# Cross-attention weighs both halves of a pair of heads in one group every second step

## The reference

```python
x = x + attn(layernorm(x), Wq, Wk, Wv, Wo)      # 32 heads of 16, 8 groups of keys, causal
x = x + xattn(layernorm(x), ctx, ctx)           # the change lies here
x = x + ffn(layernorm(x), w_gate, w_up, w_down) # 512 -> 2048 -> 512, weights -1, 0, 1, activations rounded to 8 bits

def xattn(q, k, v):            # all (4, 512, 512); 8 heads are cut from the middle axis
    qh, kh, vh = (a.reshape(32, 64, 512) for a in (q, k, v))
    qk = einsum('bdm,bdn->bmn', qh, kh) / 8
    sm = softmax(qk, axis=-1)
    return einsum('bmn,bcn->bcm', sm, vh).reshape(4, 512, 512)
```

## Time and profile before

| | |
|---|---|
| median of 3 runs | 859.85 us (857.26 to 863.59) |
| profiled execution | 858.61 us |
| its span, first to last instruction | 856.5 us |
| granted TensorE clock, mean | 0.968 |
| TensorE (PE) busy | 770.8 us, 90% |
| VectorE (DVE) busy | 658.1 us, 77% |
| ScalarE (ACT) busy | 468.2 us, 55% |
| GpSimd (POOL) busy | 412.1 us, 48% |

### The profile page before, as it was taken

One profiled execution on the slowest core, in us unless ns is written; L12 is line 12 of the kernel. 1 busy time (PEld: TensorE's weight loads), 2 busy tenths in 40 slices (PEclk: granted clock), 3 DMA queues, 4 the chain that ended last, 5 costly groups with the idle time before them and its releaser, 6 DMA issues.

```text
span 856.5 us, 14217 instructions
## 1 busy us (share of the span) xinstructions
PE 770.8 (90%) x4258; PEld 407.6 (48%) x4306; DVE 658.1 (77%) x1934; ACT 468.2 (55%) x823; POOL 412.1 (48%) x412
## 2 busy tenths in 40 slices
PE   2999679999999999998887699999996998999996
PEld 1888424444444444443665345544443343444442
DVE  7555288888898989882677787888885788889883
ACT  3556317676676767676222466666664543444451
POOL 1456379999991000001222187777787444333331
PEclk9999859999999999999999699999998999999999
DMA  7996464444342121200457455556552034443443
GB/s 257 348 329 251 131 198 117 153 148 138 128 115 55 58 61 48 72 25 20 160 191 239 134 167 159 160 168 170 158 165 59 13 69 99 98 87 87 87 86 99
DMA packets 112268, 113.61 MB, mean 133 GB/s; under 512 B 70592, under 2 KB 82496, under 8 KB 109120
## 3 DMA queue, kind: packets, MB, share of 16 engines
q1 hardware_dynamic: 105344, 91.66, 38.2%
q0 software_dynamic: 1728, 12.58, 4.3%
q10 hardware_dynamic: 5120, 8.46, 2.7%
HBM read 81.26 MB, written 20.51 MB: 119 GB/s over the span
## 4 chain that ended last, share of the span: by engine, by line
PE 16%; DVE 14%; issue 7%; POOL 5%; DMA 4%; SPq 4%; ACT 2%; DVEq 0%; ACTq 0%; POOLq 0%
PE r_pn L1235 3%; PE r_p L1278 3%; DMA r_rden<-inverse_sums 3%; POOL r_h L905 3%; DVE r_h L1097 2%; DVE r_mx L1058 2%; PE r_p L1223 2%; PE r_p L1198 2%; DVE r_stats L1024 2%; PE r_p L1224 2%; DVE r_hpart L1105 2%; PE r_pn L1294 1%; PE r_pd L1245 1%; DVE r_lo L1032 1%; DVE tok L1038 1%
## 5 line engine op out<-in xcount | busy, mean ns | idle before, releaser
L576 DVE CUSTOM_DVE_ANT_0 b_junk<-b_p,mask_qk 128x128 bf16<-128x128 f32 (+3 forms) x512 | 218.0, 484 | 35.0 <-PE b_p L601 34.8
L531 ACT ACTIVATE b_probs<-b_p 128x512 f32<-128x512 f32 (+1 forms) x352 | 176.8, 560 | 49.8 <-remote 23.8
L601 PE MATMUL b_p<-b_ks,b_qs 96*128 96x128 bf16 (+3 forms) x512 | 127.8, 314 | 19.1 <-DMA b_ks<-k_parts 11.1
L630 PE MATMUL b_p<-b_qs,b_ks 98*128 98x512 bf16 (+1 forms) x352 | 123.3, 365 | 2.0 <-DMA b_qs<-b_mrow 0.9
L948 ACT ACTIVATE r_probs<-r_p 128x512 f32<-128x512 f32 x128 | 74.3, 593 | 65.8 <-PE r_p L1224 63.7
L1058 DVE TENSOR_REDUCE r_mx<-r_p 128x1 f32<-128x512 f32 x128 | 84.9, 685 | 14.6 <-PE r_p L1198 13.4
L879 POOL TENSOR_TENSOR r_halves<-r_probs 128x1024 f32<-128x1024 f32 x32 | 76.6, 2393 | 25.6 <-ACT r_probs L948 23.2
L601 PEld LDWEIGHTS b_p<-b_ks,b_qs 96*128 96x128 bf16 x512 | 45.5, 100 | 82.8 <-DVE b_mx L576 20.0
L645 PE MATMUL b_pv<-b_probs,v 128*32 128x512 f32 (+3 forms) x1024 | 75.5, 436 | 0.0
L855 POOL MEMSET r_ql<- 64x2048 f32 x1 | 1.8, 1799 | 144.6 <-POOLq L402 144.6
L1278 PE MATMUL r_p<-wu,r_zt 128*128 128x512 bf16 x251 | 65.8, 382 | 5.0 <-DVE r_h L1097 4.8
(11 more groups left out here) (149 smaller groups left out, 1552.9 us busy)
## 6 DMA issues: line engine op xcount, KB each, us to landing
r_k<-in_ctx SPq DMA_DIRECT2D x64, 128.0 KB, 2.7
r_qh<-x_normed_high SPq DMA_DIRECT2D x64, 128.0 KB, 2.8
q_parts<-a_parts SPq DMA_DIRECT2D x16, 384.0 KB, 3.5
b_qs<-q_parts SPq DMA_DIRECT2D x32, 192.0 KB, 3.2
a_x<-in_x SPq DMA_DIRECT2D x4, 1024.0 KB, 5.6
a_wst<-in_w_gate SPq DMA_DIRECT2D x4, 1024.0 KB, 6.4
a_wst<-in_w_up SPq DMA_DIRECT2D x4, 1024.0 KB, 7.9
a_wst<-in_w_down SPq DMA_DIRECT2D x4, 1024.0 KB, 8.4
```

The source lines that it names most:

```text
L531: nc.scalar.activation(pblock(j % 2, kb)[:, j0:j0 + nj, c:c + w], p2[(NE * j + n) % BANKS2][:, 0:nj * w].rearrange("p (j c) -> p j c", j=n ...
L576: best = nc.vector.tensor_tensor_reduce(out=junk[:, 2 * ((NU * i + k) % BANKS1) + n, 0:w], in0=bank[:, c:c + w], in1=keep["mask_qk"][:, SE ...
L601: last = nc.tensor.matmul(p1_bank(i, k)[:, c:c + w], qs[0:STACK, s, j, qt * P:(qt + 1) * P], ks[0:STACK, s, 0:w], start=True, stop=True)
L630: last = nc.tensor.matmul(bank, ks[0:STACK + 2, s, kb * P:(kb + 1) * P], qs[0:STACK + 2, s, j0:j0 + nj, kb * P + c:kb * P + c + w], start= ...
```

## The change

Before, in even steps (2p + 6) TensorE sums the pair and weighs its key blocks 0 and 1, in odd steps (2p + 7) it weighs blocks 2 and 3. After, all four blocks are weighed in step 2p + 6, and odd steps weigh nothing. The same matmuls run with the same operands, into the same bank and in the same order among themselves; `weighted` is signalled at the end of step 2p + 6 in place of 2p + 7. No other engine's program changes.

```diff
-                first_half, second_half = pair_due(i, 6), pair_due(i, 7)
-                if first_half is not None:
-                    sum_probs(first_half)
-                    weigh(first_half, 0)
-                    weigh(first_half, 1)
-                if second_half is not None:
-                    weigh(second_half, 2)
-                    weigh(second_half, 3)
+                p = pair_due(i, 6)
+                if p is not None:
+                    sum_probs(p)
+                    for nb in range(KD):
+                        weigh(p, nb)
```

## The result

The changed kernel takes 874.23 us (median of 6 runs, 870.93 to 878.80) against 860.26 (6 runs, 857.26 to 863.59). The ratio is 1.0165, 95% interval 1.0124 to 1.0207: slower by 14 us. The prediction said 873.

A forecast was written before the change was run, and what follows sets the result against it. Bound: a loop per pair of steps, VectorE's maxima up to the transpose, then TensorE alone. Moved weighing 23.9 - 1.6 - 8.9 = +13.4 us on 859.85 gives 873; 8-in-10 range 861.5 to 882.

The forecast's parts named there:

- Part two: Even step's transpose of row maxima to next odd step's first score matmul: 5.01 to 6.72 us, costing 23.9 us in all.
- Part one with the y product: Odd step's first score matmul to the transpose, steps 11 to 31: 5.5 us, subtraction clear of GpSimd, saving 8.9 us.
- Part one without it: First score matmul to transpose in steps 7 and 9, before any y product: 5.0 us, saving 1.6 us.
- The end: Steps 33 to 37, transpose of step 33 to the next scores: taken as 0, about 1 us either way.
- The odd step's subtraction: Rival: VectorE's subtraction still meets GpSimd and stays slow, +20.8 us, 881; chance 0.20, including half the pairs.
- TensorE's clock: Rival: idle gaps drop TensorE to 1.2 GHz in some pairs; three such pairs give 17 us, about 890; chance 0.04.
- Hidden anyway: Rival: a VectorE and GpSimd loop of about 11.3 us covers the moved block; +0 to +4, about 862; chance 0.19.
- faster: Rival: the transpose does not hold TensorE, pairs become pure TensorE work; 7 us won, 853; chance 0.07.
- the prediction's two cases: Odd step's subtraction in steps 11 to 31 running alone, +13.4 us in total, or beside GpSimd, +20.8 us.

The follow-up runs named there:

- e2: Kernel before with three key blocks weighed in the even step and one in the odd step; 862.71 us, ratio 1.0043.
- e5: Kernel before with GpSimd's work on the sums cut (halves adds 128 of 512 columns, total two key blocks); 855.75 us, ratio 0.9943.
- e1: Kernel before with key blocks 2 and 3, the odd step's half of the weighing, left out; 862.36 us, ratio 1.0030.
- e8: Kernel before with key blocks 0 and 1, the even step's half of the weighing, left out; 852.99 us, ratio 0.9936.
- e3: Kernel before with one key block weighed in the even step and three in the odd step; 856.86 us, ratio 0.9974.

## Why the prediction was right

*Part two.* Forecast 5.01 + 1.71 = 6.72 us, measured 6.69 to 6.74 in all twelve pairs. e2 gives the same price per block, 0.85 us.

*Part one with the y product.* Forecast 5.5 us, measured 5.48 to 5.50 in steps 11 to 31. The reason given holds: GpSimd's total ended 0.8 us before the subtraction, as worked out, and e5 shows that GpSimd was the cause of the 6.26 us before.

*Part one without it.* Forecast 5.0 us for steps 7 and 9, measured 5.86 and 5.28. This term was mis-sized, because of a dependency that the prediction did not have. It named the mrow DMA as what the even step's first second_scores waits for. The trace names ScalarE's copy of kh, the high part of the context rows for the second of the two matmuls; it is a stage of step j + 2 that the list of stages ahead doesn't have. ScalarE's and TensorE's timelines of the changed kernel, steps 19 and 20:

```profile
580.83 0.62 ACT L983 ACTIVATE r_kh<-r_kk 64x512 fp32r<-64x512 f32 x1
...
581.55 0.47 PE L1223 MATMUL r_p<-r_qh,r_kk 128*128 128x512 f32 x1 [0.76 <-ACT r_kh L983]
...
582.33 0.27 PE L1207 MATMUL r_p<-ident,r_mx 128*4 128x128 f32 x1
```

The copy is written behind three exponentials of the odd step; it ends at 581.45 and the matmul starts 0.1 us later. With a y product VectorE's last maximum is later still (its row starts at 581.59, the transpose at 582.33), so it costs nothing there; without one it decides. What makes the copy late, and step 7 longer than step 9, are two DMAs of `den` that ScalarE itself issues in front of the third exponential (L974). ScalarE and its queue, then TensorE, in step 7, and behind the second mark ScalarE and its queue in step 9:

```profile
505.56 1.27 ACTq L974 DMA_DIRECT2D r_few<-r_den  x1
506.87 0.63 ACTq L974 DMA_DIRECT2D r_few<-r_den  x1
507.55 0.60 ACT L948 ACTIVATE r_probs<-r_p 128x512 f32<-128x512 f32 x1 [1.01 <-PE r_p L1224]
508.04 0.62 ACT L983 ACTIVATE r_kh<-r_kk 64x512 fp32r<-64x512 f32 x1
...
508.76 0.47 PE L1223 MATMUL r_p<-r_qh,r_kk 128*128 128x512 f32 x1 [1.42 <-ACT r_kh L983]
...
518.19 0.66 ACTq L974 DMA_DIRECT2D r_few<-r_den  x1
518.88 0.63 ACTq L974 DMA_DIRECT2D r_few<-r_den  x1
519.55 0.60 ACT L948 ACTIVATE r_probs<-r_p 128x512 f32<-128x512 f32 x1 [0.39 <-PE r_p L1224]
```

The third exponential starts 0.04 to 0.05 us behind the end of the second issue, while its scores have been there since 505.92 in step 7. The first issue took 1.27 us there and 0.66 in step 9, and the two parts one differ by 0.58 us, 5.86 and 5.28. No run moved the issues or the wait, so what that would win is open. Over the 13 intervals of part one the saving was 81.0 - 71.5 = 9.5 us against 10.5 forecast, so the stretch to step 33 grew by 23.9 - 9.5 = 14.4 and not 13.4 us.

*The end.* Forecast 0 within about 1 us; measured -1.4 from the transpose of step 33 (663.63) to the next second_scores. GpSimd's and VectorE's y product in the kernel before, then the same in the changed one, with TensorE:

```profile
650.25 2.40 POOL L879 TENSOR_TENSOR r_halves<-r_probs 128x1024 f32<-128x1024 f32 x1 [0.43 <-POOL r_total L883]
651.08 2.12 DVE L1083 TENSOR_TENSOR r_y<-r_y,r_rden 128x512 f32<-128x512 f32 x1
...
664.05 1.92 POOL L883 TENSOR_TENSOR r_total<-r_halves 128x512 f32<-128x512 f32 x1
664.15 0.67 DVE L1083 TENSOR_TENSOR r_y<-r_y,r_rden 128x512 f32<-128x512 f32 x1
...
672.06 0.80 PE L1223 MATMUL r_p<-r_qh,r_kk 128*128 128x512 f32 x1 [6.77 <-DMA r_ql<-r_mrow]
```

That is 8.43 us against 9.88. In the kernel before the y product starts 0.83 us into a `halves` of 2.40 us and ends 0.55 us after it, 2.12 us long. In the changed one it starts within 0.1 us of a `total`, takes 0.67 us, and it is GpSimd's addition that is stretched, to 1.92 us from 1.29. This is the one case in 231 in which VectorE didn't wait; the two starts are so close that VectorE seems to have come first, which the record doesn't show. The 1.45 us between the two y products are the whole difference. The prediction had seen this stretch and left it at zero; it was the same contention once more, and this time it fell on GpSimd.

*The rivals.* The odd step's subtraction stayed fast. TensorE's clock stayed at 1.00 in the changed kernel's stage, but e1 shows that the case was perhaps nearer than the 0.04 it got. Its price was too high: a pair at the lower level was to cost 5.6 us, and in e1 it cost 1.2 to 1.5, since the clock was back within nine matmuls. Hidden anyway is excluded by pairs of 12.2 us whose part two has no gap, faster by TensorE's idle time in front of the transpose. (In the sum for faster, 12 x 10.6 is 127.2 and not 127.6; nothing hangs on it.)

The two misses of 1.0 and 1.4 us have opposite signs, and the runs of the changed kernel spread over 8 us; that 873 and 874.2 are so near is partly luck.

## What to carry to other kernels

Filler work on an engine is free only where that engine waits: look for the wait that closes the loop (here the transpose for the last maximum), and put the filler in front of it, never between it and the first instruction that feeds the other engine again. Before moving work, count what each engine needs in each half of the loop. Here VectorE needs 6.27 us for part one as long as its subtraction meets GpSimd, where TensorE needs 5.76 with two blocks and 6.63 with three; from the even step's transpose to the next one VectorE needs 4.98 us (e8), where TensorE needs 5.8 with two blocks and 4.94 with one (e3). So three blocks belong in the first and one in the second, which beat the kernel before by 0.3%. And when a period changes, ask which engines' instructions will meet or miss each other afterwards; here the prediction's two cases lay 7.4 us apart on that question, of 23.9 us of moved work. No run has the changed kernel with a stretched subtraction in its odd steps, so this size is an estimate; e5 shows 0.5 us of it in each pair.

## What the runs showed of the hardware

A VectorE subtraction of 64 x 512 elements takes 0.69 us alone. Started while a GpSimd addition runs, it ends 0.55 us after that addition (0.53 to 0.57 in 230 of 231 cases, the y products among them): 1.47 us with 0.92 left of the addition, 1.66 with 1.11. It is a wait for the other's instruction to end, not a slower rate.

A DMA that ScalarE issues holds back the ScalarE instruction behind it: the exponential starts 0.04 to 0.05 us after the end of the second issue, of 0.63 us, in steps 7, 9 and 19 of the changed kernel.

Leaving out a seventh of TensorE's work in a pair (e1: busy 9.37 us against 10.93) brought its clock down to the 1.2 GHz level in five of twelve even steps and cost 1.2 to 1.5 us each time: a kernel that does less was not faster. In front of one of these were gaps of 1.10, 0.30 and 0.50 us in close succession; gaps of 1.14 and 0.73 us in another pair of e1 did not do it, nor did 0.32 and 0.76 us in each pair of the changed kernel. What makes the difference was not tried.
